# Sparse attention of a two-layer decoder by query tiles, with four heads per score matmul

## The reference

```python
x = _layernorm(x + _L0_attn_ref(x, ...))      # recurrent
x = _layernorm(x + _L0_xattn_ref(x, ctx_1024, ...))
x = _layernorm(x + _L0_ffn_ref(x, ...))       # 8 experts, one per token
x = _layernorm(x + _L1_attn_ref(x, ...))      # sparse self-attention
x = _layernorm(x + _L1_xattn_ref(x, ctx_1024, ctx_1024, ...))  # cross attention
x = _layernorm(x + _L1_ffn_ref(x, ...))       # 8 experts, two per token

# _L1_attn_ref: 16 heads of 8 features, 256 queries, 256 keys
strided = cols % 128 >= 128 - 8
local = cols[None, :] // 128 == rows // 128
layout = (strided[None, :] | local) & (cols[None, :] <= rows)
scores = jnp.where(layout, einsum('bhqd,bhkd->bhqk', q, k) * scale, finfo.min)
out = einsum('bhqk,bhkd->bhqd', softmax(scores), v)  # then @ W_proj + b_proj
```

## Time and profile before

| what | value |
|---|---|
| median of 3 runs | 1335.23 us (1333.54 to 1335.52) |
| profiled execution | 1334.87 us, of which the span is 1332.8 us |
| PE, DVE, ACT, POOL busy | 88%, 55%, 52%, 12% of the span |
| sparse attention, second pass | 463.18 to 508.74 us |
| cross attention, second pass | 517.47 to 649.76 us |

### The profile page before, as it was taken

How to read it: one execution, slowest core, us unless ns; L and a number is a source line. 1 busy time by engine, 2 the same in 40 slices (tenths; PEclk the granted TensorE clock), 3 DMA queues, 4 the chain that set the end, 5 groups by cost and what they waited for, 6 DMA issues and landing times.

```text
span 1332.8 us, 21891 instructions
## 1 busy us (share of the span) xinstructions
PE 1178.3 (88%) x7325; PEld 773.1 (58%) x7325; DVE 736.7 (55%) x1890; ACT 697.5 (52%) x1881; POOL 153.9 (12%) x272
## 2 busy tenths in 40 slices
PE   3789989998889998999798999899879999899957
PEld 2563875554765585555485467555467548555536
DVE  5541655667643375657754256566865336555551
ACT  3460765554553285555455157555545418655523
POOL 4310210001120120000212012000022002100000
PEclk9899999999899999999899999999989999999989
DMA  7300000000000000000000000000000000000000
GB/s 232 94 1 0 1 0 1 25 1 1 1 11 1 0 0 1 1 25 1 1 2 10 1 0 1 1 1 25 1 1 9 1 0 0 1 1 1 1 1 8
DMA packets 21058, 15.53 MB, mean 12 GB/s; under 512 B 872, under 2 KB 18645, under 8 KB 20957
## 3 DMA queue, kind: packets, MB, share of 16 engines
q1 hardware_dynamic: 20956, 14.24, 3.7%
HBM read 13.18 MB, written 1.05 MB: 11 GB/s over the span
## 4 chain that ended last, share of the span: by engine, by line
issue 57%; PE 30%; DVE 3%; POOL 3%; ACT 3%; POOLq 1%; SPq 1%; DVEq 0%; DMA 0%; ACTq 0%
PE ps L711 9%; PE ps L783 4%; PE ps L745 3%; PE ps L751 3%; PE ps L803 2%; PE ps L791 2%; POOL rstd L1424 2%; PE ps L724 1%; PE ps L613 1%; PE ps L779 1%; PE ps L646 1%; POOLq L1423 1%; PE ps L695 1%; SPq L440 1%; DVE lg_nmax L1706 1%
## 5 line engine op out<-in xcount | busy, mean ns | idle before, releaser
L1075 ACT ACTIVATE arena<-ps 128x512 f32<-128x512 f32 (+6 forms) x304 | 171.1, 573 | 267.8 <-PE ps L875 207.6
L1856 DVE TENSOR_REDUCE nmax<-ps 128x1 f32<-128x512 f32 x256 | 164.5, 686 | 128.5 <-PE ps L864 128.5
L1266 ACT ACTIVATE arena<-ps,nmax 128x512 f32<-128x512 f32 x256 | 174.3, 686 | 8.0 <-DVE nmax L1856 8.0
L875 PEld LDWEIGHTS ps<-ident,arena 128*128 128x128 f32 x1024 | 109.6, 141 | 110.7 <-issue 63.7
L875 PE MATMUL ps<-ident,arena 128*128 128x128 f32 x1024 | 151.8, 284 | 24.5 <-ACT arena L1266 24.4
L1861 DVE COPY arena<-ps 128x512 f32<-128x512 f32 x128 | 87.7, 685 | 57.3 <-PE ps L875 57.0
L711 PE MATMUL ps<-big,w1a 128*128 128x512 f32 x256 | 117.3, 604 | 0.0
L1235 ACT ACTIVATE arena<-ps,snm 128x136 f32<-128x136 f32 x256 | 91.7, 374 | 5.8 <-DVE snm L1786 5.8
L1422 POOL TENSOR_TENSOR vare<-mv,eps_ln 128x2 f32<-128x2 f32 x64 | 13.4, 209 | 691.0 <-DVE mv L1535 690.6
L711 PEld LDWEIGHTS ps<-big,w1a 128*128 128x128 f32 x256 | 46.3, 189 | 57.5 <-issue 56.5
L783 PE MATMUL ps<-kT,arena 128*128 128x136 f32 x512 | 77.2, 279 | 0.0
(11 more groups left out here) (350 smaller groups left out, 2140.1 us busy)
## 6 DMA issues: line engine op xcount, KB each, us to landing
ctx<-in_ctx_dram SPq DMA_DIRECT2D x4, 512.0 KB, 4.1
w1a<-in_L_ffn_W_dram SPq DMA_DIRECT2D x1, 2048.0 KB, 9.7
w1b<-in_L_ffn_W_dram SPq DMA_DIRECT2D x1, 2048.0 KB, 11.6
w2b<-in_L_ffn_W_dram SPq DMA_DIRECT2D x8, 256.0 KB, 6.2
X<-in_x_dram SPq DMA_DIRECT2D x4, 256.0 KB, 2.9
out_dram<-Y SPq DMA_DIRECT2D x4, 256.0 KB, 2.4
arena<-in_L_xattn_Wq_dram SPq DMA_DIRECT2D x1, 512.0 KB
arena<-in_L_xattn_Wk_dram SPq DMA_DIRECT2D x1, 512.0 KB
```

The lines of the kernel that those rows point to most:

```text
L875: last = pe.transpose(ps[:, 4 + h, k * P:(k + 1) * P], cprob[:, h, k * P:(k + 1) * P], ident[:, :])
L1075: return act.activation(dst, src, ACT.Copy)
L1266: act.activation(cprob[:, h, :], bank(2 * (t % 2) + h), ACT.Exp, bias=nmax[:, s:s + 1], accum_out=rsum[:, j % 2, s:s + 1]).then_inc(c_exp, 1)
L1856: dve.tensor_reduce(nmax[:, s:s + 1], bank(s % 4), AX.X, ALU.max, negate=True)\
```

## The change

Sparse attention now goes by query tile `t` and "quads" of four heads. Features of four heads are 32 rows of `qT` and `kT`. DVE makes four masked copies of the keys (`kTm[:, i]` holds the rows of head i of each quad), so one f32 matmul with the 32 rows of queries of a quad as weights and the four copies as 512 moving columns gives the scores of four heads; the causal mask is put under it by a bf16 matmul of 512 columns. Two quads stand side by side in `two_quads`, with different 32-row slices of the PE array. Values work in 32-column slices, four quads of a tile next to each other. Exponentials are 128 wide. ACT keeps only the exponentials; the copies out of PSUM go to DVE. The shared keys have their own small score matmuls, and their exponentials and sums are handled for all heads at once. The masked keys and values lie in the memory of the first mixture's weights `w1a`, which SP loads anew (2 MB) behind each sparse stage but the last. The stage is written out, with no hardware loop.

```diff
-                def scores(hh, u):
-                    pe.wait_ge(qm_ready, it * NH + 2 * hh + u + 1)
...
-                        pe.matmul(ps[:, o, 0:QT * KW], ident_bf[:, :], sparse[:, :], start=True, stop=False)
+                def two_quads(n):
+                    for q in (2 * n, 2 * n + 1):
+                        pe.matmul(bank(q % QUADS), ident_bf[:, :], causal[:, :].unsqueeze(1).to_broadcast([P, QH, P]),
+                                  start=True, stop=False)
+                    for q in (2 * n, 2 * n + 1):
+                        t = q // QUADS
+                        pe.matmul(bank(q % QUADS), qT[strip(q), t * P:(t + 1) * P],
+                                  kTm[strip(q), :, t * P:(t + 1) * P], start=False, stop=True).then_inc(s_ps, 1)
...
+                def turn_probs(q):
+                    pe.wait_ge(s_exp, it * NQ + q + 1)
+                    if q == 0:
+                        pe.wait_ge(gs_read, it + 1)
+                    if q >= 2:
+                        pe.wait_ge(sT_ready, it * NQ + q - 1)
...
+                    for i in range(QH):
+                        for q in range(t * QUADS, (t + 1) * QUADS):
+                            last = pe.matmul(ps[strip(q), 6, t * P:(t + 1) * P], Vm[:, i, t, strip(q)],
+                                             spT[:, q % 6, i, :], start=(i == 0), stop=(i == QH - 1 and t % QT == 0))
...
+                    turn_probs(2 * n)
+                    turn_probs(2 * n + 1)
+                    if n + 2 < NQ // 2:
+                        two_quads(n + 2)
+                    if n and n % 2 == 0:
+                        values(n // 2 - 1)
...
             def sparse_attention(it):
-                turn_x(it, 3, 3)
+                turn_x(it, 3, 3, wait=False)
+                values_read(it, 1, 1)
+                project_v(3, 6, 0)
+                pe.wait_ge(xT_ready, it * 5 + 3)
                 keys_read(it, 4, 1)
                 values_read(it, 3, 0)
...
                 for n in range(NQ // 2):
+                    turned(2 * n)
+                    if n + 2 < NQ // 2:
+                        row_max(2 * n + 4)
...
+                    turned(2 * n + 1)
+                    if n + 2 < NQ // 2:
+                        row_max(2 * n + 5)
```

The second part is ACT's queue in cross attention, where the next tile's exponentials move ahead of the copy and of the small work:

```diff
                     for t in range(TT):
+                        nj, nt = (j, t + 1) if t + 1 < TT else (j + 1, 0)
+                        act.wait_ge(cT_ps, it * (NS * PAIRS) + j * NS + 2 * t + 1)
+                        if nj < PAIRS:
+                            exps(nj, nt, 0)
                         act.wait_ge(cT_ps, it * (NS * PAIRS) + j * NS + 2 * t + 2)
                         copy(cprobT[:, 2 * (t % 2) + 1, :], bank(5)).then_inc(cT_odd, 1)
-                        nj, nt = (j, t + 1) if t + 1 < TT else (j + 1, 0)
                         if nj < PAIRS:
-                            exps(nj, nt, 0)
+                            exps(nj, nt, 1)
                         if t == 0 and j:
                             spread(j - 1, 7)
                         if t == 1 and j + 1 < PAIRS:
                             queries(j + 1)
```

More of the change, by code:

```diff
@@ L27 @@
 CB = 8
-KW = CB + P
+QUADS, QH = 4, 4
+NQ = TOK // P * QUADS
 XH, DK = 16, 64
@@ L807, in two_heads, with strip @@
[L807 to L820 removed]
+                def strip(q):
+                    return slice((q % QUADS) * 32, (q % QUADS + 1) * 32)
@@ new lines, in shared_scores @@
+                def shared_scores():
+                    for b in range(GROUP):
+                        t = b * QT + 1
+                        for q in range(QUADS):
+                            k0 = b * SEQ + P - CB
+                            last = pe.matmul(ps[:, 4 + q, b * QH * CB:(b + 1) * QH * CB],
+                                             qT[strip(q), t * P:(t + 1) * P], kTm[strip(q), :, k0:k0 + CB],
+                                             start=True, stop=True)
+                    last.then_inc(gs_ps, 1)
@@ L826, in sparse_attention @@
+                two_quads(1)
                 pe.wait_ge(v_ready, it + 1)
-                add_zeros(True, False)
-                with pe.Fori(0, NH // 2 - 1) as hh:
-                    two_heads(hh, True)
-                two_heads(NH // 2 - 1, False)
-                pe.wait_ge(g_ready, it + 1)
-                for b in range(GROUP):
-                    last = pe.transpose(ps[:, 4, b * P:(b + 1) * P], G[:, b, :, :], ident[:, :])
-                last.then_inc(gT_ps, 1)
+                shared_scores()
@@ L837, in sparse_attention @@
+                for n in range(NQ // 2):
+                    if n in SHARED_AT:
+                        turn_shared(SHARED_AT.index(n))
+                    turn_probs(2 * n)
[4 more added lines that the diff above has]
+                        values(n // 2 - 1)
+                values(TT - 1)
+                pe.wait_ge(rs_ready, it + 1)
                 for t in range(TT):
-                    last = pe.transpose(ps[:, 5, t * P:(t + 1) * P], O[:, t, :], ident[:, :])
+                    last = pe.transpose(ps[:, 0, t * P:(t + 1) * P], O[:, t, :], ident[:, :])
@@ new lines, in shared_exps, with shared_turned @@
+                def shared_exps(b):
+                    act.wait_ge(g_arg, it * GROUP + b + 1)
+                    act.activation(G[:, b, :, :], G[:, b, :, :], ACT.Exp).then_inc(g_exp, 1)
+                def shared_turned(b):
+                    act.wait_ge(gT_ps, it * GROUP + b + 1)
+                    copy(GT[:, b, :], ps[:, 7, b * P:(b + 1) * P]).then_inc(gT_ready, 1)
+                for q in range(NQ):
+                    exps(q)
+                    if q == NQ // 2 - 1:
+                        shared_exps(0)
+                    if q == NQ - 3:
+                        shared_exps(1)
+                    if q == NQ // 2 + 1:
+                        shared_turned(0)
```

270 lines of the change are left out of this document (124 added, 146 removed).

## The result

| kernel | median | runs |
|---|---|---|
| before, timed beside it | 1335.38 us (1333.54 to 1337.05) | 4 |
| changed | 1322.68 us (1321.64 to 1323.63) | 4 |

The ratio is 0.9905, with a 95% interval of 0.9888 to 0.9922: 12.7 us faster. The forecast was 1302 us, 33 less, with a range of 1290 to 1323. The direction was right and the time lies at the upper edge of the range, but less than half of the gain came.

The account below looks back on a forecast made before the run. PE was taken to bound the sparse loop and cross attention. Terms summed to -7.7 us a pass, -30.8 for four, and -2.3 more in the last: -33, giving 1302 us from 1334.87, range 1290 to 1323.

Parts of the forecast that it names:

- Products of 32 rows: Sparse scores: a pair of 32-row products takes 1.04 us, so `two_quads` with its two masks costs 1.48 us.
- Values in 32-column slices: Sparse values: four slices run side by side, 1.03 us a tile; about 1.9 if only two do.
- rivals 1, 4 and 5: Values overlap only in twos, +2.6 us/pass (0.13 including pairs); no 32-wide overlap, +11.1 (0.08); no values overlap, +8.6 (0.03).
- Loop: Sparse stage, first to last transposes: 3.7 tiles of 7.1 us, 26.4 us instead of 32.4, -6.0 a pass.
- Front: Sparse stage, transposes of X to first transposes of probabilities: 11.5 us against 8.07, +3.5 a pass.
- End: Sparse stage, last transposes to output projection: 5.1 us against 5.08, counted as 0.
- Rival 2: Sparse tile: PE-DVE chain longer, PSUM emptied too slowly, tile stays 8.7 us; +6 a pass, 1326 us; chance 0.08.
- The filler at line 773: Sparse front: a projection moved into the wait for `XT` gives nothing there and costs 0.65 us.
- Cross attention: ACT's even exponential ahead of the odd copy: -0.6 us a pair, -3.3 per pass, -5.6 in the last.
- The new wait for the queries: Cross attention: PE waits some 0.3 us for the next pair's later scaled queries, ahead of `project_out`.
- Rival 3: Cross attention: ACT's new order does nothing, late queries giving back the gain; +15.5 us, 1318 us; chance 0.1.
- Reload of `w1a`: 2 MB loaded behind the last sparse values, needed a cross attention later (132 us): cost 0.

Follow-up runs that it names:

- e4: Kernel before with only ACT's new exponential order in a cross attention pair; 1319.32 us, ratio 0.9877.
- e5: Changed kernel with idle PE work, transposes of the identity, ahead of PE's waits throughout the sparse stage; 1308.91 us, ratio 0.9797.
- e11: Changed kernel with idle identity transposes only before quads 14 and 15, the last values and the output projection; 1314.72 us, ratio 0.9843.
- e9: Changed kernel with DVE's copies before maxima, shorter front, scaled queries before the odd exponential, and identity transposes in PE's waits; 1280.88 us, ratio 0.9591.
- e2: Changed kernel with both DVE copies of a quad pair ahead of both row maxima; 1306.76 us, ratio 0.9782.
- e10: Same as e9 but without any idle transposes in PE's waits; 1288.26 us, ratio 0.9642.
- e7: Changed kernel with DVE's copies before maxima, a shorter front, and identity transposes in PE's waits, none before quad 1; 1293.92 us, ratio 0.9681.
- e3: Changed kernel with ACT's old order in a cross attention pair; 1341.55 us, ratio 1.0042.
- e1: Changed kernel with idle f32 identity products on PE ahead of its waits in the sparse stage; 1332.58 us, ratio 0.9976.

## Why the prediction was wrong

The measured time is 20.3 us over the forecast (1322.7 against 1302.4, which is 33 under 1335.4).

- **The step that failed** is none of the terms, but what all of them took for granted: that PE runs at clock 1.00 in the stage because it did so before. The change took 9 us of work a pass from PE (the busy column: 32.1 in the second pass after, 41.0 in e4, whose stage is that of before), left it with a dozen waits of 0.3 to 1.5 us a pass, and I named a lower clock only among the signs of a wrong prediction, with no rival, no price and no chance. It cost about 15.6 us (estimate from e5), of which half or more was the stage of pass 4.
- **Products of 32 rows**: forecast 1.48 for `two_quads`, measured 1.58. The products were right (1.06 a pair for 1.04); the two masks took 0.52 where 0.44 was taken (476.59 to 477.11 to 478.17). Six of them lie between first and last transposes: 0.6.
- **Values in 32-column slices**: forecast 1.03 a tile, measured 1.01. All four slices overlap, so rivals 1, 4 and 5 fall.
- **Loop**: forecast 26.4, measured 27.2; besides `two_quads` there are the last quads, which wait 0.96 and 0.74 for exponentials and had no term. **Front**: 11.5 forecast, 11.8 measured. **End**: 5.1 forecast; 5.35 in e5 at full clock (492.78 to 498.13), 6.3 in the second pass of the changed kernel, whose clock falls there. These three are 1.35 us a pass, 5.4 in all, and pass 1 of e11 (42.15 against 40.9) says the same. With the clock's 15.6 that makes 21.0 for a miss of 20.3, which is as close as such an estimate comes.
- **Rival 2**, a longer chain between PE and DVE: the wait was where it had been put, and 1.12 as laid out (0.9 to 1.2). It did not grow, so a tile took 7.2 us (476.12 to 483.29) for the 7.1 laid out.
- **The filler at line 773** gave nothing, as forecast: PE waits 0.69 for ACT's copy of that projection.
- **Cross attention**: forecast -15.5, alone -15.8 (e4). In the changed kernel the stage lengths gave 12.9: the last pairs of a pass have waits too, and the clock falls there (0.82 in the last 9.6 us of pass 4, 1.00 in e5; the stage 124.66 us there and 123.04 in e5). The new wait for the queries was forecast at 0.3 and is 0.37, and with the queries first it is gone and pass 4 3.1 us shorter still (e9). Rival 3 falls.
- **Reload of `w1a`**: 0, as forecast: the first mixture, which uses `w1a`, did not grow. From its first matmul behind `turn_x` to the query projection of the sparse stage it is 51.76 us in the second pass, and was 51.86 (412.82 to 464.68).

That the time lies inside the range at all, by 0.3 us, is luck: the range had been widened for rivals that did not happen.

On the clock, the Trainium skill, TensorE: Matmul & The Clock Gate, section A second HAM failure mode: psum-queue depth-cycling, describes a kernel in which PE's short idle stretches between groups of matmuls make the clock go back and forth between its levels, and throughput falls with it. This case's trace agrees: PE's waits are 0.3 to 1.5 us and the granted clock of a stage is 0.76 to 0.96. The Trainium skill, TensorEngine Tiling (Array Packing), section PSUM Bottleneck, warns that the emptying of PSUM may become the limit when tiling makes TensorE faster. This case's trace agrees in part. In the changed kernel PE did wait for a copy out of PSUM, 1.12 us before an odd quad, but for its place in DVE's queue and not its length, since the same copies in e2's order took that wait away. Then ACT's exponentials, which read the scores out of PSUM, were what PE waited for, 0.54 at a time.

What stays open: why the clock fell at the front only in pass 4 of the changed kernel, though the wait of 1.50 us is there in every pass (in e2 it fell there in pass 2 and not in pass 4). The runs show that filling the waits ends it, not what decides between two like passes.

## What to carry to other kernels

When a change takes work from TensorE and leaves it waiting, price the clock as a term of its own: find the new waits, and ask what the work behind them costs at the lower clock (here 2.07 us for products of 1.13). If such a kernel's time scatters from run to run, or like passes differ in length with the same instructions, read the granted clock of each pass first; transposes of the identity into unused PSUM columns, no longer than the waits and counted from a row that shows their true length, are a cheap test and may stay as a remedy. Then go for the waits themselves: e10, with shorter waits and no filler, took 1288 us, e5 with fillers 1309.

## What the runs showed of the hardware

- The same wait of 0.74 us before the second quad's transposes was followed by the lower clock in the second pass of e7 (four transposes in 1.03 us) and not in the first (0.66).
- The lower clock followed waits of only 0.74 us (e7) to 1.50 us (changed kernel), and with the waits filled by transposes the clock was 1.00 in all four sparse stages of the profiled run of e5.
- The same program, e3, took from 1331 to 1350 us with a mean clock of 0.966 to 0.941.
- An f32 product of 128 columns shows as two instructions and took 0.22 us (e1, nine in 2.01), a transpose of the same size as one and 0.11 (e5, where twelve in a row last 1.47 and eight 1.04).
- Sixteen products with 32 output columns each (32 instructions) took 1.01 us at full clock and 1.86 at the lower (changed kernel, passes 2 and 4).
